# Turning the gated rows by DMA through DRAM instead of on TensorE, in a Mamba-2 block on one core

## What is computed

```python
proj = jnp.einsum('bsd,ed->bse', x, in_proj_w)
gate = proj[..., :INTER]                       # INTER = 128 heads * 64 = 8192
hBC = proj[..., INTER:INTER + CONV_DIM]        # causal conv over 4 tokens, then silu
...
Y_diag = jnp.einsum('bzlhn,bzshn,bhzls,bzshp->bzlhp', Cc, Bc, L, xch)
...
Y = (Y_diag + Y_off).reshape(b, s, H, P) + hs * D[None, None, :, None]
y = Y.reshape(b, s, INTER)
g = y * jax.nn.silu(gate)
gg = g.reshape(b, s, G, INTER // G)            # G = 8 groups of 1024 channels
var = jnp.mean(gg * gg, axis=-1, keepdims=True)
gg = gg * jax.lax.rsqrt(var + EPS)
out = gg.reshape(b, s, INTER) * norm_w
return jnp.einsum('bsi,oi->bso', out, out_proj_w)
```

## Time and profile before

| | |
|---|---|
| median of 3 runs | 1656.82 us (1656.03 to 1657.55) |
| span of the profiled execution | 1654.4 us |
| PE busy | 98% |
| DVE busy | 82% |
| POOL busy | 81% |
| ACT busy | 74% |
| granted PE clock | 0.9 or more in every slice |
| DMA | 265 MB, q1 53.4% of 16 engines |

### The profile page before, as it was taken

The page is one execution under the profiler, slowest core; times in us unless marked ns, Lnnn a source line. Parts: engine busy times, 40 slices in busy tenths (PEclk is TensorE's granted clock), DMA queues, the critical chain, the costliest instruction groups (busy, mean ns, idle before and its releaser), DMA issues.

```text
span 1654.4 us, 31767 instructions
## 1 busy us (share of the span) xinstructions
PE 1617.2 (98%) x10792; PEld 1301.3 (79%) x10792; DVE 1364.4 (82%) x1675; ACT 1232.1 (74%) x2625; POOL 1341.4 (81%) x1238
## 2 busy tenths in 40 slices
PE   7999999999999999999999999999999999999998
PEld 5778878878787877878778787887878787787776
DVE  5978788887979878788788988888788887879787
ACT  5267787777877777777877778777786877777775
POOL 3148689886998779897798968988698977989797
PEclk9999999999999999999999999999999999999999
DMA  3253366553665546564675535655466465655464
GB/s 126 66 190 116 103 185 198 176 163 108 197 185 166 156 150 193 159 165 135 169 209 169 170 115 178 189 172 170 124 195 185 146 170 141 195 162 172 129 180 141
DMA packets 232528, 265.46 MB, mean 160 GB/s; under 512 B 156073, under 2 KB 157617, under 8 KB 228145
## 3 DMA queue, kind: packets, MB, share of 16 engines
q1 hardware_dynamic: 232368, 263.45, 53.4%
HBM read 162.20 MB, written 69.73 MB: 140 GB/s over the span
## 4 chain that ended last, share of the span: by engine, by line
PE 62%; POOL 13%; DVE 8%; ACT 8%; issue 6%; DMA 2%; SPq 0%; ACTq 0%; DVEq 0%; POOLq 0%
PE P L257 7%; PE P L259 7%; PE P L258 7%; PE P L466 5%; PE P L476 5%; PE P L341 4%; PE P L334 4%; PE P L335 4%; PE P L477 4%; PE P L483 4%; ACT P L579 3%; PE P L491 3%; DVE hsX L784 2%; POOL AL L1081 2%; POOL xch L1106 2%
## 5 line engine op out<-in xcount | busy, mean ns | idle before, releaser
L579 ACT ACTIVATE P<-AB,SC 128x128 f32<-128x128 f32 x1016 | 305.9, 364 | 0.0
L257 PE MATMUL P<-xh,AH 128*128 128x512 f32 x656 | 267.9, 408 | 1.9 <-DVE xl L885 1.9
L784 DVE SCALAR_TENSOR_TENSOR hsX<-P,cwt,hsX 128x1023 f32<-128x1023 f32 x189 | 241.8, 1280 | 25.6 <-ACT hsX L516 21.1
L259 PE MATMUL P<-xh,AL 128*128 128x512 f32 x656 | 257.2, 392 | 0.0
L258 PE MATMUL P<-xl,AH 128*128 128x512 f32 x656 | 255.5, 389 | 0.0
L749 ACT ACTIVATE sq<-yb 128x512 bf16<-128x512 f32 x128 | 80.8, 631 | 214.3 <-DVE yb L1048 214.3
L1081 POOL TENSOR_TENSOR AL<-AR,AH 128x512 fp32r<-128x512 f32 x82 | 115.4, 1408 | 134.0 <-ACT AH L503 134.0
L476 PE MATMUL P<-OH,gTh 128*128 128x512 f32 x512 | 214.6, 419 | 2.5 <-DVE al L1061 1.5
L334 PE MATMUL P<-GH,xh 128*128 128x512 f32 x512 | 200.7, 392 | 0.2 <-ACT GH L548 0.2
L335 PE MATMUL P<-GH,xl 128*128 128x512 f32 x512 | 200.2, 391 | 0.0
L477 PE MATMUL P<-OH,gTl 128*128 128x512 f32 x512 | 200.2, 391 | 0.0
(11 more groups left out here) (214 smaller groups left out, 4143.1 us busy)
## 6 DMA issues: line engine op xcount, KB each, us to landing
AB<-acr_d SPq DMA_DIRECT2D x128, 512.0 KB, 4.9
half_d<-hsX SPq DMA_DIRECT2D x60, 512.0 KB, 3.6
AR<-in_wa SPq DMA_DIRECT2D x80, 256.0 KB, 2.9
TS<-in_wg SPq DMA_DIRECT2D x16, 1024.0 KB, 7.0
TS<-in_wo SPq DMA_DIRECT2D x16, 1024.0 KB, 6.6
part_d<-pl SPq DMA_DIRECT2D x64, 256.0 KB, 3.0
pl<-part_d SPq DMA_DIRECT2D x64, 256.0 KB, 2.6
al<-acc_d SPq DMA_DIRECT2D x64, 256.0 KB, 3.0
```

What stands on the lines that cost most here:

```text
L257: te.matmul(o, ah_, bh_, start=(first and i == 0), stop=False)
L259: r = te.matmul(o, al_, bh_, start=False, stop=(last and i == n - 1))
L579: r = se.activation(decays(m)[:, h, :], AB[m % 2][:, h, :], ACT.Relu, bias=SC[s % 2][:, c, 3, h:h + 1], scale=-1.0)
L784: ve.scalar_tensor_tensor(out=o[:, d:T], in0=raw[:, 0:T - d], scalar=cwt[:, n, 3 - d:4 - d], in1=o[:, d:T], op0=ALU.mult, op1=ALU.add).the ...
```

## The change

For slots 8 to 126 PE no longer turns the gated rows. Instead

1. DVE writes the rows of slots 8 and up into one of two buffers in the free half of `hsX` (`rows_of`), not into `yb`;
2. ACT copies them, behind the square, into two planes of 16-bit halves (`planes`);
3. SP stores the planes in DRAM (`gate_d`, 256 KB) at the start of the next slot, and issues a turning load into `GTd` near the end of that slot, behind `AB`;
4. the output product of slot `j` stands in PE's slot `j + 2` (`out_slot`), and so do `gTh` and `gTl`, which now read SBUF, in ACT's and DVE's slot `j + 1`;
5. for slabs from the second on, `OH` is made in the slab's second slot instead of its first, `OL` one slot later too, and the gate's weights, `SC` and `EA` are loaded in the fourth instead of the third slot.

Slots 0 to 7 and slot 127 stay with PE. The semaphores `x_in` and `sct_st` become one list `x_sct`.

```diff
+    def by_pe(j):
+        return j < 8 or j == M - 1
+
+    def out_slot(j):
+        return j + 1 if by_pe(j) else j + 2
+
+    outs_of = {m: [j for j in range(M) if out_slot(j) == m] for m in range(M + 2)}
...
+        planes = [hsX[0][:, 0, 512 * i:512 * i + 512].bitcast(u16).rearrange("p (b t) -> p b t", b=2) for i in range(2)]
+        GTd = [hsX[0][:, 1, 512 * i:512 * i + 512] for i in range(2)]
+        ybs = [hsX[0][:, 2, 512 * i:512 * i + 512] for i in range(2)]
...
-                if m < M:
+                if m < M and by_pe(m):
                     banks_free("GTr", m)
                     te.wait_ge(s_g, m + 1)
...
+                    if not by_pe(m):
+                        if m >= 10:
+                            se.wait_ge(gate_st[m % 2], 16 * nturn(m - 2))
+                        se.activation(planes[m % 2], rows_of(m).bitcast(u16).rearrange("p (t b) -> p b t", b=2), ACT.Copy).then_inc(s_pln, 1)
                 if m + 1 < M:
                     se.wait_ge(s_gt, m + 2)
                     se.activation(tg[:, :], bank("GT", m + 1), ACT.Tanh, scale=0.5).then_inc(s_tg, 1)
+                for j in outs_of[m + 1]:
+                    if by_pe(j):
+                        se.wait_ge(s_gtr, ngtr(j))
+                    else:
+                        se.wait_ge(gate_in[j % 2], 16 * nturn(j))
+                    if j:
+                        se.wait_ge(s_o, j)
+                    se.activation(gTh[:, :, :], turned_rows(j), ACT.Copy).then_inc(s_gth, 1)
...
-                    if c == 0:
+                    if c == (1 if s else 0):
                         se.wait_ge(s_ts3, s + 1)
                         se.wait_ge(ts_in, 16 * (3 + 2 * s))
...
+        def sp_planes(j):
+            sp.wait_ge(s_pln, j - 7)
+            if j >= 10:
+                sp.wait_ge(gate_in[j % 2], 16 * nturn(j - 2))
+            sp.dma_start(gate_d[j % 2], planes[j % 2]).then_inc(gate_st[j % 2], 16)
+
+        def sp_gate_turned(j):
+            sp.wait_ge(gate_st[j % 2], 16 * nturn(j))
+            if j >= 10:
+                sp.wait_ge(s_gtl, j - 1)
+            sp.dma_start_transpose(GTd[j % 2].bitcast(u16).rearrange("p (k r) -> p k r", k=4),
+                                   gate_d[j % 2].rearrange("t b c -> (t b) c")).then_inc(gate_in[j % 2], 16)
+
+        def sp_partials(j):
+            c = j % 8
+            if j // 8 % 2:
+                sp.wait_ge(acc_st[c], 16 * (j // 8 + 1))
+                sp.wait_ge(acc_st[(j - 2) % 8], 16 * ((j - 2) // 8 + 2))
+                sp.dma_start(pl[c % 2][:, :], part_d[c]).then_inc(pl_in[c % 2], 16)
+                sp.dma_start(al[c % 2][:, :], acc_d[c]).then_inc(al_in[c % 2], 16)
...
+                if m and not by_pe(m - 1):
+                    sp_planes(m - 1)
...
+                if m:
+                    for j in outs_of[m - 1]:
+                        sp_store(j)
+                for j in outs_of[m + 1]:
+                    if j < M - 1:
+                        sp_partials(j)
...
                     if m + 3 < M:
                         sp_rows(m + 3)
+                if m and not by_pe(m - 1):
+                    sp_gate_turned(m - 1)
+                if m < M:
                     for k in slot_halves[m + 1]:
                         if k % 2:
                             sp_ring(k // 2 + 6)
```

More of the change, by code:

```diff
@@ L99, in ngl, with ngtr, nturn @@
         return 4 * (1 + s) if s < 2 else 8 + 3 * (s - 1)
+    def ngtr(m):
+        return m + 1 if m < 8 else 9
+    def nturn(j):
+        return (j - 8) // 2 + 1
     def nsa(m):
@@ L186, in decays, with rows_of @@
             return E[:, :, :] if m else EM[0][:, :].rearrange("p (h l) -> p h l", h=8)
-        x_in = [sem(f"x_in{i}") for i in range(NC)]
+        def rows_of(m):
+            return yb[:, :] if m < 8 else ybs[m % 2]
+        x_sct = [sem(f"x_sct{i}") for i in range(NC)]
         cst_in, prm_in, ts_in, acr_st, eal_st = (
@@ L193, in mamba_moe_block_kernel @@
         acc_st = [sem(f"acc_st{i}") for i in range(NC)]
-        sct_st = [sem(f"sct_st{i}") for i in range(NC)]
         rows_in = [sem(f"rows_in{i}") for i in range(2)]
@@ L200, in mamba_moe_block_kernel @@
         ht_in = [sem(f"ht_in{i}") for i in range(2)]
+        gate_st = [sem(f"gate_st{i}") for i in range(2)]
+        gate_in = [sem(f"gate_in{i}") for i in range(2)]
         s_hi, s_lo = sem("high_half"), sem("low_half")
@@ L244, in pair, with turned_rows @@
             return P[:, b0:b0 + 2, :].rearrange("p b n -> p (b n)")
+        def turned_rows(j):
+            return (bank("GTr", j) if by_pe(j) else GTd[j % 2]).rearrange("p (k t) -> p k t", k=4)
         def banks_free(kind, i):
@@ L468, in pe_program @@
                     r.then_inc(s_y, 1)
[L469 to L473 removed]
+                for j in outs_of[m]:
+                    banks_free("O", j)
+                    te.wait_ge(s_gtl, j + 1)
+                    so = j // 8
+                    o = bank("O", j)
                     te.wait_ge(s_oh, 4 * so + 4)
@@ L1201, in pool_program @@
                             pool_ring(k // 2 + 4)
-                if m and (m - 1) // 8 % 2 and (m - 1) // 8 < NS - 1:
-                    n_, r = ngc(m - 1), (m - 1) % 2
+                for j in outs_of[m]:
+                    if j // 8 % 2 == 0 or j // 8 == NS - 1:
+                        continue
+                    n_, r = ngc(j), j % 2
                     pe_.wait_ge(s_alo, n_)
@@ L1332, in sp_program @@
                         sp.dma_start(TS[:, :, :], wo[s + 1]).then_inc(ts_in, 16)
-            sp_store(M - 1)
+            for j in outs_of[M]:
+                sp_store(j)
             for c in range(NC):
```

119 lines of the change are left out of this document (56 added, 63 removed).

## The result

The changed kernel takes 2017.84 us (2016.95 to 2019.31, four runs), beside 1657.18 us (1656.03 to 1658.41) of the kernel before: a ratio of 1.2174, interval 1.2159 to 1.2189. That is slower by 361 us, where 32 us slower was forecast; it is also far past rival 3's 1760 us.

The account below looks back on a forecast made before the run. PE's instruction stream was taken as the bound, DVE and ACT close behind. 1656.8 - 61 (turns) + 88 (odd slabs) - 5 (last odd slab) + 10 (even slabs) = 1689 us; range 1604 to 1735, the forecast's own 1660 to 1735.

Parts of the forecast that it names:

- rival 3: SP's loop itself becomes the bound, turning load late in every slot: about 1760 us, chance 0.10.
- the direct term: PE's wait for OH at an odd slab's first output product: 5 us, bounds 2.5 to 7, eight slabs.
- 0.4 us for the planes' store: SP's added time per slot for issuing the store of the planes: 0.4 us.
- the lateness of 5.7 us: ACT's wait for the turning load in slot 57; in even slabs 2.5 us, mostly absorbed, costing 1.5 us a slab.
- the test by which to know it: If even slabs wait as much as odd ones, rival 3 holds and the fetch of partial sums isn't the cause.
- 4.7 taken: Time from issue to landing of the new turning load behind AB: 4.7 us, bounds 3.1 and 6.6.
- the copy at 0: ACT's copy into planes, 1.06 us a slot, costs PE nothing to 0.4 us; 0 in the sum.
- the gain of 61: Turns leaving PE: 119 groups at 0.43 us, 51 us, plus 10 us of waits in front of them.
- `gTl` from SBUF: ACT and DVE splitting the turned rows from SBUF instead of PSUM: costs nothing.
- Following by two slots: Output product two slots behind instead of one: one slot more in the path, 11.6 us; no separate cost in the sum.
- 0.4 was forecast: Slots in the middle of even slabs become 0.4 us shorter, a sign to look for in the new trace.

Follow-up runs that it names:

- e1: Changed kernel with copy, store and turning load kept, but gTh and gTl splitting unturned rows so nobody waits for the load: 1715.36 us, ratio 1.0343.
- e3: Changed kernel with the turning load of gated rows issued right behind the halves' load, ahead of store, fetches, weights and AB: 1760.53 us, ratio 1.0623.
- e14: Changed kernel with unturned rows split, ACT's copy into planes kept, store and turning load dropped: 1704.44 us, ratio 1.0287.
- e13: Kernel before without any turns, gTh and gTl reading yb as it lies, output product still one slot behind: 1622.0 us, ratio 0.9766.
- e6: Kernel before with only one of the four turns of gated rows made per slot, from slot 1 on: 1635.37 us, ratio 0.9853.
- e4: Changed kernel with the output product three slots behind instead of two: 1737.37 us, ratio 1.0476.
- e9: Changed kernel, output product four slots behind, ACT's copy moved to the next slot before its wait for gated rows, store and load one slot later: 1704.01 us.
- e2: Changed kernel with unturned rows split and ACT's copy, store and turning load all dropped, product two slots behind: 1646.96 us, ratio 0.9929.
- e11: Changed kernel with ACT's gTh, and its wait for the load, moved to the end of ACT's slot: 1912.42 us, ratio 1.1541.
- e15: Changed kernel with the turning load issued early in SP's queue and gTh moved to the end of ACT's slot: 1810.3 us, ratio 1.0922.

## Why the prediction was right and wrong

**Right: the sign, and the kind of wait in the slot worked.** In the second slot of odd slabs ACT waits for the load and PE for `OH`: forecast 5.7 and 5 us, measured 5.60 and 5.21 in slot 57, the first by two misses that cancel (issue 1.3 us earlier against ACT, landing 1.2 us longer); `PE P L501 <- ACT OH L800` has 52.1 us in 10 waits, the 5 us of the direct term. SP's order there was read rightly as well: from the ring load to the turning load's issue it is 972.31 to 979.73 us, 7.4, against 6.7 plus 0.4 for the planes' store; but that store held SP 1.50 us and AB 0.43 instead of 1.30, which cancel too.

**Wrong first: "In even slabs ... the lateness of 5.7 us shrinks to 2.5, which the waits of ACT mostly take up."** Forecast 1.5 us an even slab; measured 12 to 19 us of growth, net of what the missing turns give back. The prediction treated lateness as something that a slot passes on to PE once, and that ACT's idle time absorbs. It isn't absorbed: ACT's waits before the square, which should have taken it up, are 247.9 us where they were 214.3. ACT's `gTh` stands in front of `AH` and the high half, on which POOL waits, on which SP's queue waits, and the load stands last in that queue. So SP moves back with ACT, and the lateness that the load has by its place is paid again in the next slot with a ring load. The prediction had this loop, as rival 3, with a chance of 0.10, and it had the test by which to know it, that even slabs wait as much as odd ones. They wait less than half as much (94 us and 221), so by that test neither account is whole: the fetch of the sums is a large part, and the load is late without it too. e1, without the wait, gave back 303 us, and e3, which moves the load in SP's queue and changes neither a byte nor an operation, 257: that shows that the load's place and the wait for it are the cause. That the loop renews the wait is shown by the rows from slot 59 to 60 and by the slots with and without a ring load; its own share of the 303 us isn't.

**Wrong second: rival 3's size.** It counted a loop of 14 us: 6.7 of SP, 4.7 of landing and 2.5 of ACT. Measured between two issues from slot 59 to 60 it was 19.5 us. The landing was 7.8 us there, and 5.9 in the median, against 4.7 taken (bounds 3.1 and 6.6). Its median is 1.2 us above my value, whose model was one load behind 512 KB; the new load stands behind AB in every slot, and the turning load of halves takes longer as well now (4.5 us in the median, before 3.7). Which part of the added traffic does this no run tells. SP was held for 4.90 us by the issue of that one load; the longest issue in the earlier trace rows is 1.30 us. And I let the loop exist only in the 64 odd slots, at 3 us each, less what overlaps; there are 81 waits of 3.9 us in the mean, 315 us, which is about what the waiting costs (303).

**Wrong third: the copy at 0.** "What hides it is that the gate is only needed after the next projection half" overlooked that the next slot's `Off` uses the gate's bank, so that bank must be read, not only filled, before. 0.5 us a slot, where I had allowed 0.4 as the bound; 59 us in all (e14).

**Wrong fourth: the gain of 61.** Without the turns PE isn't the only bound: e13 gives 39 of 66 (for its 128 groups), with DVE at 86% and POOL at 85% busy, and `gTl` from SBUF takes 998 ns instead of 682, which the prediction put at nothing. e6 gives 24 us for three turns of four in 127 slots, where three quarters of 0.43 us would be 41. The 0.43 us a slot is what PE loses locally, and about 60% of it was to be had. Following by two slots, at nothing in the sum, takes 27 back. Slots in the middle of even slabs are shorter by 0.2 us (52, 68) where 0.4 was forecast.

On the way itself: four turns on PE last 274 ns each, the load that replaces them 5.9 us, with a store of 3.6 us ahead of it. At two slots behind that wasn't hidden; at three it was (e4), and the change still lost 79 us. The Trainium skill's rule that the prediction weighed (VectorE: DVE Perf Modes, Rules for kernel authors: on TensorE where PSUM will do) points the way that these runs went.

**What stays open**: the loop's own share of the 303 us; why following two slots behind instead of one costs 27 us; what holds e9 at +47 us when nobody waits for the load; why the traffic costs 25 us in one setting and 9 in the other. No version with the whole computation was faster than the kernel before; the ones that were (e2, e6, e13) leave turns out.

## What to carry to other kernels

When a change puts a DMA's landing in front of an engine, follow that engine's later instructions until they reach the queue that issues the DMA: if they do, the wait isn't paid once, but again in each slot in which the queue waits for that engine. On one in-order queue a load that someone waits for belongs ahead of those that nobody needs soon; that place alone was worth 257 us here. And moving work off a full engine onto one with idle time is free only where that idle time lies: a copy of 1.04 us, 119 times, cost 59 us in front of the Tanh, and in e9, where ACT was waiting anyway, some 32 us less.

## What the runs showed of the hardware that I had not expected

- **A turning load behind queued DMAs.** The same 256 KB land in 3.3 us (median of 119, e3) when issued behind the halves' load and the wait for the planes, and in 5.9 us (at most 9.6) when issued right behind AB's 512 KB. SP is held by its issue for 1.2 to 5.1 us, median 1.4:

```profile
L1314 SPq DMA_TRANSPOSE hsX<-gate_d x119: 1232/1397/5060, 240.6 to 1995.4; - x119
```

- **DVE with both inputs in SBUF beside a busy POOL.** The same subtraction of 128x512 took 682 ns in the mean with one input in PSUM; with both in SBUF 847 to 998 in most runs (944 in e2, 998 in e13), 1114 in e11, 1261 in e15, but 755 in the kernel after. What POOL does at that moment sorts them:

| run | inputs of `gTl` | POOL idle throughout: ns (count) | POOL busy throughout: ns (count) |
|---|---|---|---|
| before | PSUM, SBUF | 683 (31) | 681 (64) |
| e13 | both SBUF | 685 (31) | 1158 (83) |
| e1 | both SBUF | 685 (34) | 1055 (56) |
| after | both SBUF | 689 (66) | 853 (13) |
| e11 | both SBUF | 692 (32) | 1365 (40) |

  So it isn't SBUF as such that costs, but SBUF for both inputs while POOL works. The Trainium skill (VectorE: DVE Perf Modes, Two Vector instructions with no wait between them) says that the second SBUF input of a Vector instruction is read through an interface that GpSimd shares; these numbers agree with that.
- **PE's clock behind a wait.** After waits of 2.25 us (1032.24) and 5.21 us (988.79) matmuls came every 0.43 us for some 3 to 6 us and then every 0.23. Filling the waits raised the mean granted clock from 0.945 to 0.975 and changed nothing in the time.
